# Last attention: moving the softmax divisors' reciprocals, their multiply from VectorE to GpSimd, and the first batch's output products by one group

## The chip, the cores and the metric

The kernel runs on one core of one Trainium2 chip. The time is the device time of one execution in microseconds (us); lower is better. Before the change three runs gave 2289.3, 2290.64 and 2291.68 us, median 2290.64.

## The reference

The program is a stack of four gated blocks, each a cross-attention and a feed-forward stage, on x of shape (2, 1024, 256). The change lies in the attention of the last block. There the roles are turned round: x, normalised, is the set of latents that asks, and the context (64 rows a batch) and x together are what is asked.

```
xn = layer_norm(x, ln_media_w, ln_media_b)      # the context, 2 x 64 x 256
zn = layer_norm(latents, ln_lat_w, ln_lat_b)    # x, 2 x 1024 x 256
q = (zn @ Wq).reshape(b, Nz, H, Dh)             # H = 8 heads, Dh = 64
kv_in = jnp.concatenate([xn, zn], axis=1)       # 1088 keys
k, v = kv_in @ Wk, kv_in @ Wv
sim = jnp.einsum('bhqd,bhfd->bhqf', q * scale, k)
alphas = jax.nn.softmax(sim, axis=-1)
out = jnp.einsum('bhqf,bhfd->bhqd', alphas, v)
return out.reshape(b, Nz, H * Dh) @ Wout
x = x + jnp.tanh(g_xattn[3]) * (that output)
```

## The kernel before, in words

The kernel has no scheduler: each engine has its own function, written in the order in which it runs, and semaphores tie them together. The last attention is `pe_xattn3` (TensorE), `act_xattn3` (ScalarE), `dve_xattn3` (VectorE) and `pool_xattn3` (GpSimd).

The work is cut into 16 groups G = 0 to 15. A group is one pair of heads p = G // 2 % 4 of one batch b = G // 8, for one half h = G % 2 of its 1024 queries (`block3`). A group has nine steps j = 0 to 8, one for each 128 keys (the last has 64). In a step:

- TensorE computes the scores of 128 keys by 512 queries for both heads (`pe_scores3`), a precise product in which the low parts of keys and queries take part, and the value product of the step two back (`pe_values3`), which gathers in bank 4. It also makes a rough product for the next group (`pe_rough3`), of which only the row maxima are used. The rough products of a group all use banks 5 and 6, so each waits until VectorE has reduced the one before (`s_ar`, line 2019).
- ScalarE takes the exponential (`act_weigh3`, line 2061), four buffers in turn.
- GpSimd adds the exponentials of the nine steps up (`pool_sum3`, lines 2089 and 2092): a step's sum starts when its exponential is there.
- VectorE reduces the rough product (`dve_rough3`, line 2019). At step 8 it makes the group's negated maxima out of them (`dve_maxima3`: line 2024, then two small multiplies at line 2026). TensorE turns those round (side work "m", "128x65" matmuls) before it can finish the next group's scores.

Beside this each step may carry one piece of side work, named by `side3(G, j)` and executed by all engines at that step: "s" at step 1 sums the exponentials of group G - 1 over the keys in bank 7, so that each query's divisor stands in every row, and ScalarE copies it to `x3_SM`; "q" at step 2 makes queries; "k" in even groups and "v" in odd ones at steps 3 to 5 make the next keys or values; "m" at step 8; "o" at steps 6 and 7 multiplies the finished outputs of a batch half by Wout, adds them to x and takes the statistics of the next layer norm. "q" and "k" bring VectorE two subtractions each, the low parts (line 1965); step 5 of an even group has short ones.

The divide is `dve_divide3`. `x3_RC` takes the reciprocals of group G - 1's divisors in four quarters of 128 columns, at steps 2 to 5 of group G (line 2074), and after the fourth one multiply of 128 x 512 elements scales the outputs in `x3_OE` in place (line 2080). Its semaphore `s_on` lets ScalarE write the next divisors and lets "o" start. "o" stands in groups 7, 8 and 15, each for the group before it, and after group 15 for group 15 itself.

VectorE's instructions at a step stand in this order: side work, rough reduce, reciprocal quarter, multiply. So what the multiply waits for, the next step's rough reduce waits for too, and behind it TensorE's next rough product.

Of the kernel before, what the change touches and what calls it, by code (L numbers as in the profile page):

```python
# [77 lines left out]
def build(nc, d, out):  # L78
    with ExitStack() as ctx:
# [647 lines left out]
        o = oR  # L727
# [1050 lines left out]
        def act_mid(e):  # L1778
            act_heads(e, 2)
            e.wait_ge(s_mk, 2)  # L1780
            for i in range(NT + 9):
# [32 lines left out]
                if 17 <= i < 23 and STAGES >= 7:  # L1814
# [14 lines left out]
        s_one = sem("ones_rows")  # L1829
        s_am, s_ar = sem("rough_scores"), sem("rough_maxima")  # L1830
        s_pa, s_oc = sem("keys_summed"), sem("values_kept")
        FIRST3 = [("k", 0, 0), ("k", 0, 1), ("q", 0, 0), ("v", 0, 0), ("v", 0, 1), ("q", 1, 0), ("k", 0, 2), ("v", 0, 2),
                  ("m", 0, 0)]
        FIRST_BANK3 = (0, 1, 2, 3, 0, 1, 7, 4, 7)

        def side3(G, j):

            n = G // 2
            if j == 1 and G:
                return ("s", G - 1, 0)  # L1840
            if j == 2 and G + 2 < 16:
                return ("q", G + 2, 0)
            if 3 <= j <= 5 and n + 1 < 8:
                return ("v" if G % 2 else "k", n + 1, j - 3)
            if 6 <= j <= 7 and G >= 7 and (G - 1) // 2 % 4 == 3:
                return ("o", G - 1, j - 6)
            if j == 8 and G + 1 < 16:
                return ("m", G + 1, 0)
            return None
# [70 lines left out]
        def act_side3(e, s):  # L1920
            kind, a, c = s
            if kind == "o":
                return
            bk = SIDE3_BANK[s]
            e.wait_ge(s_mi, SIDE3_AT[s] + 1)
            if kind == "k":
                for x in range(2):
                    e.activation(x3_K1[high3(x), a % 2, x, keys3(c)], psum[high3(x), bk, 0:512 if c < 2 else 64],
                                 ACT.Copy).then_inc(s_mo, 1)
                for x in range(2):  # L1930
                    e.wait_ge(s_mo, SIDE3_KEPT[s] - 3 + x)
                    e.activation(x3_K1[high3(1 - x), a % 2, x, keys3(c)], x3_K1[high3(x), a % 2, x, keys3(c)],
                                 ACT.Copy).then_inc(s_mo, 1)
            elif kind == "v":
                if c < 2:
                    m = e.activation(x3_VF[:, a % 2, 4 * c:4 * c + 4, :].rearrange("p x n -> p (x n)"), psum[:, bk, :],
                                     ACT.Copy)
                else:
                    m = e.activation(x3_VF[0:64, a % 2, 8, :], psum[0:64, bk, 0:128], ACT.Copy)
                m.then_inc(s_mo, 1)  # L1940
            elif kind == "q":
                for x in range(2):
                    e.activation(x3_Q1[high3(x), a % 3, x, :], psum[high3(x), bk, :], ACT.Copy).then_inc(s_mo, 1)  # L1943
                for x in range(2):
                    e.wait_ge(s_mo, SIDE3_KEPT[s] - 3 + x)
                    e.activation(x3_Q2[high3(x), a % 3, x, :], x3_Q1[high3(x), a % 3, x, :], ACT.Copy).then_inc(s_mo, 1)
            elif kind == "m":
                e.activation(x3_Q2[0:64, a % 3, 1, :], psum[0:64, bk, :], ACT.Copy).then_inc(s_mo, 1)
            else:
                if a:  # L1950
                    e.wait_ge(s_on, 40 + a)
                e.activation(x3_SM, psum[:, bk, :], ACT.Copy).then_inc(s_mo, 1)

        def dve_side3(e, s):
# [111 lines left out]
            e.wait_ge(s_pv, 40 + 9 * G + 9)  # L2066
            e.activation(x3_OE[:, p, 512 * h:512 * h + 512], psum[:, 4, :], ACT.Copy).then_inc(s_oc, 1)

        def dve_divide3(e, G, i):

            b, p, h = block3(G)
            if i == 0:
                e.wait_ge(s_mo, SIDE3_KEPT["s", G, 0])
            m = e.reciprocal(x3_RC[:, 128 * i:128 * i + 128], x3_SM[:, 128 * i:128 * i + 128])
            if i == 3 or (G, i) == (15, 1):
                c = slice(0, 512) if G < 15 else slice(128 * i - 128, 128 * i + 128)
                settle(e, dve, m)
                e.wait_ge(s_oc, G + 1)
                ov = x3_OE[:, p, 512 * h + c.start:512 * h + c.stop]
                e.tensor_tensor(ov, ov, x3_RC[:, c], ALU.mult).then_inc(s_on, 1)  # L2080

        def pool_sum3(e, G, j):
            g, rows = 9 * G + j, 128 if j < 8 else 64
# [69 lines left out]
        def dve_xattn3(e):  # L2153
# [8 lines left out]
            for G in range(16):  # L2162
                for j in range(9):
                    if j == 0 and G + 1 < 16:
                        dve_rough3(e, G + 1, 0)
                    if j == 8 and G + 1 < 16:
                        dve_maxima3(e, G + 1)
                    if side3(G, j):
                        dve_side3(e, side3(G, j))
                    if j < 8 and G + 1 < 16:  # L2170
                        dve_rough3(e, G + 1, j + 1)
                    if 2 <= j <= 5 and G:
                        dve_divide3(e, G - 1, j - 2)
            for i in range(4):
                dve_divide3(e, 15, i)
            for s in SIDE3[-2:]:
                dve_side3(e, s)

        def pool_xattn3(e):
# [7 lines left out]
            for G in range(16):  # L2187
                for j in range(1, 9):
                    pool_sum3(e, G, j)
                if G in (7, 8, 15):  # L2190
                    for i in range(2):
                        for t in tiles3(G - 1, i):
                            pool_rstd(e, 113 + t + 1, t)
            for i in range(2):
                for t in tiles3(15, i):
# [448 lines left out]
```

## Time and profile before

| | |
|---|---|
| median of three runs | 2290.64 us |
| the profiled execution's own time | 2299.54 us |
| its span, first to last instruction | 2297.6 us |
| TensorE matmul / weight load busy | 1812.1 us (79%) / 1123.4 us (49%) |
| VectorE busy | 1199.5 us (52%) |
| ScalarE busy | 879.3 us (38%) |
| GpSimd busy | 836.2 us (36%) |
| mean granted TensorE clock | 0.876 |
| the 16 groups of the last attention | from 1468.6 to some 2038 us |

The span is what the timeline is laid out on; the execution's own time is 1.9 us longer. It lies 0.4% over the median of the timed runs. A timeline row gives the start of an instruction (or of a merged run of like ones), how long it took, the engine, the line, what it writes and reads with shapes, how many were merged, and in square brackets how long its engine had been idle and whose end released it. fp32 matmuls appear as two instructions each. TensorE's ends are modelled; the distance from start to start is the reliable figure.

### The profile page before, as it was taken

The page shows a single profiled execution, that of the slowest core. Times are in us where ns is not written, and L with a number is a line of the kernel's source. Part 1 is how long each engine was busy: PE and PEld are TensorE (multiplying, and loading weights), DVE is VectorE, ACT ScalarE, POOL GpSimd, SP SyncE. Part 2 cuts the span into 40 slices and gives each one's busy share as a digit, 9 for nine tenths or more (in the row PEclk, how much of TensorE's full clock was granted, in tenths as well). Part 3 has the DMA queues.
Part 4 walks back from the last instruction along what each step waited for, and adds up shares of the span by engine and source line. Part 5 has one row for each costly group of instructions (what it writes and reads, how often), then busy time and mean ns, then how long its engine had stood idle before and what let it go on. Part 6 is the DMA issues. An engine that isn't in the chain of part 4 may idle for free.

```text
span 2297.6 us, 25602 instructions
## 1 busy us (share of the span) xinstructions
PE 1812.1 (79%) x9072; PEld 1123.4 (49%) x9072; DVE 1199.5 (52%) x2089; ACT 879.3 (38%) x1365; POOL 836.2 (36%) x805
## 2 busy tenths in 40 slices
PE   6744999818875788883997787899998999976895
PEld 3334889705653322262554355444454544463553
DVE  5932554354768467741113688555655565542334
ACT  3112443203236777720121455454553345410440
POOL 2133000062457444432001454555554555625014
PEclk9756999959977799985999888899998999977997
DMA  9112332120000000051112000000000000012343
GB/s 368 48 67 72 115 107 81 47 65 1 1 18 1 1 1 1 1 220 47 37 37 86 24 1 1 28 1 1 1 1 0 1 1 1 0 74 82 93 133 92
DMA packets 60075, 112.22 MB, mean 49 GB/s; under 512 B 7829, under 2 KB 51288, under 8 KB 57520
## 3 DMA queue, kind: packets, MB, share of 16 engines
q1 hardware_dynamic: 52272, 90.02, 11.2%
q0 software_dynamic: 7680, 20.57, 2.8%
q8 instruction: 76, 1.25, 0.2%
q14 instruction: 47, 0.39, 0.1%
HBM read 71.12 MB, written 39.80 MB: 48 GB/s over the span
## 4 chain that ended last, share of the span: by engine, by line
PE 61%; DVE 17%; POOL 8%; issue 5%; ACT 5%; DMA 2%; another core or an unknown queue 1%; SPq 0%; POOLq 0%; DVEq 0%; ACTq 0%
PE psum L149 57%; POOL arena L1519 2%; ACT arena L1318 2%; POOL arena L723 2%; POOL xb L718 2%; DVE arena L2080 2%; DVE arena L2019 1%; DVE arena L154 1%; PE psum L183 1%; DVE arena L164 1%; DVE arena L460 1%; DMA arena<-xb 1%; DVE arena L1400 1%; POOL arena L620 1%
## 5 line engine op out<-in xcount | busy, mean ns | idle before, releaser
L149 PE MATMUL psum<-arena 128*128 128x512 f32 (+20 forms) x5127 | 1230.0, 469 | 193.5 <-DVE arena L1434 30.6
L149 PEld LDWEIGHTS psum<-arena 128*128 128x128 f32 (+6 forms) x5127 | 603.7, 172 | 710.3 <-issue 471.2
L149 PE MATMUL psum<-rounded 128*128 128x270 f32 (+6 forms) x2688 | 486.8, 335 | 50.9 <-DVE arena L2019 24.4
L149 PEld LDWEIGHTS psum<-rounded 128*128 128x128 f32 (+3 forms) x2688 | 380.1, 188 | 162.1 <-DVE arena L2019 55.8
L2092 POOL TENSOR_TENSOR arena<-arena 128x1024 f32<-128x1024 f32 (+1 forms) x112 | 267.7, 2390 | 172.4 <-ACT arena L2061 170.7
L723 POOL DMA_INDIRECT arena<-yb,arena x80 | 78.3, 979 | 410.4 <-DMA yb<-arena 364.6
L2061 ACT ACTIVATE arena<-psum 128x1024 f32<-128x1024 f32 x144 | 147.2, 1022 | 208.4 <-PE psum L149 207.7
L2019 DVE TENSOR_REDUCE arena<-psum 128x1 f32<-128x1024 f32 x128 | 156.2, 1222 | 98.1 <-PE psum L149 96.9
L1318 ACT ACTIVATE arena<-psum,arena 128x1024 f32<-128x1024 f32 (+1 forms) x192 | 156.3, 909 | 46.4 <-PE psum L149 46.3
L1535 POOL TENSOR_TENSOR arena<-arena 128x256 f32<-128x256 f32 x128 | 94.1, 758 | 129.8 <-ACT arena L1318 129.0
L718 POOL DMA_INDIRECT xb<-arena x80 | 80.3, 1004 | 115.2 <-DVEq L2385 38.1
L191 ACT ACTIVATE arena<-psum 128x512 f32<-128x512 f32 x56 | 31.7, 596 | 215.2 <-PE psum L183 215.2
L183 PE MATMUL psum<-arena 128*128 128x128 f32 x224 | 42.7, 339 | 82.3 <-DVE arena L964 53.7
L759 DVE SCALAR_TENSOR_TENSOR rounded<-arena,rounded 128x540 fp32r<-128x540 f32 (+1 forms) x96 | 82.0, 886 | 33.6 <-ACT rounded L889 32.2
L883 ACT ACTIVATE arena<-psum,arena 128x540 f32<-128x540 f32 x64 | 45.4, 710 | 129.7 <-PE psum L149 126.9
L159 POOL TENSOR_SCALAR arena<-arena 128x1 f32<-128x1 f32 x113 | 24.4, 216 | 172.2 <-DVE arena L155 166.5
L183 PEld LDWEIGHTS psum<-arena 128*128 128x128 f32 x224 | 34.8, 187 | 91.1 <-DVE arena L964 54.2
L1965 DVE SCALAR_TENSOR_TENSOR rounded<-psum,rounded 64x512 fp32r<-64x512 f32 (+1 forms) x80 | 47.2, 590 | 60.5 <-ACT rounded L1943 47.4
L164 DVE TENSOR_SCALAR arena<-arena 128x256 f32<-128x256 f32 x128 | 61.3, 495 | 24.5 <-POOL arena L160 23.5
L2089 POOL TENSOR_TENSOR arena<-arena 128x1024 f32<-128x1024 f32 x16 | 38.0, 2377 | 84.3 <-ACT arena L2061 84.3
L160 POOL TENSOR_TENSOR arena<-arena 128x1 f32<-128x1 f32 x113 | 63.0, 557 | 9.4
L957 DVE TENSOR_TENSOR arena<-psum,arena 128x256 f32<-128x256 f32 (+1 forms) x40 | 16.9, 422 | 94.8 <-PE psum L149 94.8
(245 smaller groups left out, 1869.1 us busy)
## 6 DMA issues: line engine op xcount, KB each, us to landing
arena<-in_w SPq DMA_DIRECT2D x8, 2048.0 KB, 8.1
yb<-arena SPq DMA_DIRECT2D x102, 128.0 KB
xb<-arena SPq DMA_DIRECT2D x5, 2048.0 KB, 17.4
arena<-xb SPq DMA_DIRECT2D x70, 128.0 KB, 2.2
arena<-in_w1u SPq DMA_DIRECT2D x4, 2048.0 KB, 14.8
arena<-xb SPq DMA_DIRECT2D x8, 512.0 KB
arena<-in_w1d SPq DMA_DIRECT2D x1, 4096.0 KB, 13.8
arena<-in_w3b SPq DMA_DIRECT2D x1, 4096.0 KB, 12.4
```

The source lines that it names most:

```text
L149: return e.matmul(o, l, r, start=start, stop=stop, skip_group_check=True)
L160: e.tensor_tensor(RS[:, t:t + 1], VE[:, t:t + 1], cst("nhalf")[:, 0:1], ALU.pow).then_inc(s_rs, 1)
L164: e.tensor_scalar(xn(t), src(t), MV[:, t, 0:1], RS[:, t:t + 1], ALU.subtract, ALU.mult).then_inc(s_xn, 1)
L183: m = e.transpose(pt[:, t, k, :], src(2 * i + t)[:, 128 * k:128 * k + 128], ident)
L718: e.indirect_dma_start(buf, bass.IndirectOffsetOnAxis(idx[:, c:c + 1], 0), src(c % NT), None, bounds_check=bound, oob_is_err=False).then_i ...
L723: e.indirect_dma_start(dst, None, buf, bass.IndirectOffsetOnAxis(idx[:, col:col + 1], 0)).then_inc(s_gth[s], 16)
L759: e.scalar_tensor_tensor(out=dst, in0=src, scalar=1.0, in1=hi, op0=ALU.mult, op1=ALU.subtract).then_inc(sig, 1)
L1318: e.activation(PT[:, u % 3, 2 * h:2 * h + 2, 0:n], psum[:, bk:bk + 2, 0:n], ACT.Exp, bias=NBD[:, 0:1]).then_inc(s_ae, 1)
L1535: e.tensor_tensor(PT[:, u % 3, 2 * h:2 * h + 2, 0:128], PT[:, u % 3, 2 * h:2 * h + 2, 0:128], bc(cst("caus"), 1, 2), ALU.mult).then_inc(s_ ...
L2019: m = e.tensor_reduce(x3_MX[:, t, a, 0:1], psum[:, bk:bk + 2, :].rearrange("p c n -> p (c n)"), AX.X, ALU.max)
L2061: e.activation(x3_P[0:rows, g % 4].rearrange("p a n -> p (a n)"), psum[0:rows, bk:bk + 2, :].rearrange("p a n -> p (a n)"), ACT.Exp, scale ...
L2092: m = e.tensor_tensor(ac, ac, x3_P[0:rows, g % 4], ALU.add)
```

## The change

Three things are done. First, the quarters of the reciprocals are placed by a small table, `quarters3`: in odd groups at steps 3, 4, 5 and 6, in even groups one at step 5, two at step 6, one at step 7, in group 15 at steps 2 to 5. They are issued after the step's rough reduce as before, and each raises a new semaphore `s_rc3`. Second, the 128 x 512 multiply of groups 0 to 14 is done by GpSimd, after its sum of step 7 (in group 15 after that of step 5), when all four quarters and the values are there; GpSimd's sum of step 8 stands behind it. ScalarE may write the next divisors as soon as the quarters are made. The last group's divide stays on VectorE in two halves. Third, "o" for groups 6 and 7 stands in groups 8 and 9 and no longer in 7 and 8; that for group 14 stays in group 15.

```
-            if 6 <= j <= 7 and G >= 7 and (G - 1) // 2 % 4 == 3:
-                return ("o", G - 1, j - 6)
+            if 6 <= j <= 7 and G in (8, 9, 15):
+                return ("o", G - 1 if G == 15 else G - 2, j - 6)
...
-                    e.wait_ge(s_on, 40 + a)
+                    e.wait_ge(s_rc3, 4 * a)
...
+        def quarters3(G, j):
+
+            if G == 15:
+                return [j - 2] if 2 <= j <= 5 else []
+            if G % 2:
+                return [j - 3] if 3 <= j <= 6 else []
+            return [0] if j == 5 else [1, 2] if j == 6 else [3] if j == 7 else []
+
+        def dve_divisors3(e, G, i):
+
             if i == 0:
                 e.wait_ge(s_mo, SIDE3_KEPT["s", G, 0])
+                if G:
+                    e.wait_ge(s_on, 40 + G)
+            e.reciprocal(x3_RC[:, 128 * i:128 * i + 128], x3_SM[:, 128 * i:128 * i + 128]).then_inc(s_rc3, 1)
+
+        def pool_divide3(e, G):
+
+            b, p, h = block3(G)
+            e.wait_ge(s_rc3, 4 * G + 4)
+            e.wait_ge(s_oc, G + 1)
+            ov = x3_OE[:, p, 512 * h:512 * h + 512]
+            e.tensor_tensor(ov, ov, x3_RC, ALU.mult).then_inc(s_on, 1)
...
-                    if 2 <= j <= 5 and G:
-                        dve_divide3(e, G - 1, j - 2)
-            for i in range(4):
-                dve_divide3(e, 15, i)
+                    if G:
+                        for i in quarters3(G, j):
+                            dve_divisors3(e, G - 1, i)
+            for i in range(2):
+                dve_divisors3(e, 15, 2 * i)
+                dve_divisors3(e, 15, 2 * i + 1)
+                dve_divide3(e, i)
...
                 for j in range(1, 9):
                     pool_sum3(e, G, j)
-                if G in (7, 8, 15):
+                    if G and j == (5 if G == 15 else 7):
+                        pool_divide3(e, G - 1)
+                if G in (8, 9, 15):
```

VectorE's order in an even group (group 4), from the low parts of step 3 to the maxima, before:

```order
L1965 SCALAR_TENSOR_TENSOR rounded<-psum,rounded 64x512 x2
L2019 TENSOR_REDUCE arena<-psum 128x1
L2074 RECIPROCAL arena<-arena 128x128
L1965 SCALAR_TENSOR_TENSOR rounded<-psum,rounded 64x64 x2
L2019 TENSOR_REDUCE arena<-psum 128x1
L2074 RECIPROCAL arena<-arena 128x128
L2080 TENSOR_TENSOR arena<-arena 128x512
L2019 TENSOR_REDUCE arena<-psum 128x1 x2
L2024 TENSOR_REDUCE arena<-arena 128x8
L2026 TENSOR_SCALAR arena<-arena 128x4 x2
```

and after the change (here L1966 is the low parts, L2020 the rough reduce, L2084 a quarter of the reciprocals, L2025 and L2027 the maxima):

```order
L1966 SCALAR_TENSOR_TENSOR rounded<-psum,rounded 64x512 x2
L2020 TENSOR_REDUCE arena<-psum 128x1
L1966 SCALAR_TENSOR_TENSOR rounded<-psum,rounded 64x64 x2
L2020 TENSOR_REDUCE arena<-psum 128x1
L2084 RECIPROCAL arena<-arena 128x128
L2020 TENSOR_REDUCE arena<-psum 128x1
L2084 RECIPROCAL arena<-arena 128x128 x2
L2020 TENSOR_REDUCE arena<-psum 128x1
L2084 RECIPROCAL arena<-arena 128x128
L2025 TENSOR_REDUCE arena<-arena 128x8
L2027 TENSOR_SCALAR arena<-arena 128x4 x2
```

The multiply is gone from between the rough reduces; three of the quarters now stand behind it, and one between the last rough reduce and the maxima.

GpSimd's order in groups 14 and 15 before:

```order
L2089 TENSOR_TENSOR arena<-arena 128x1024
L2092 TENSOR_TENSOR arena<-arena 128x1024 x6
L2092 TENSOR_TENSOR arena<-arena 64x1024
L2089 TENSOR_TENSOR arena<-arena 128x1024
L2092 TENSOR_TENSOR arena<-arena 128x1024 x6
L2092 TENSOR_TENSOR arena<-arena 64x1024
```

and after (L2109 and L2112 are the sums, L2092 the multiply):

```order
L2109 TENSOR_TENSOR arena<-arena 128x1024
L2112 TENSOR_TENSOR arena<-arena 128x1024 x6
L2092 TENSOR_TENSOR arena<-arena 128x512
L2112 TENSOR_TENSOR arena<-arena 64x1024
L2109 TENSOR_TENSOR arena<-arena 128x1024
L2112 TENSOR_TENSOR arena<-arena 128x1024 x4
L2092 TENSOR_TENSOR arena<-arena 128x512
L2112 TENSOR_TENSOR arena<-arena 128x1024 x2
L2112 TENSOR_TENSOR arena<-arena 64x1024
```

The multiply stands before the last sum of a group, in group 15 before the last three.

## Rows read from the trace of the kernel before

**Rows 1.** Waits from 1465 to 2035 us: total us, times, longest.

```profile
PE psum L149 <- DVE arena L2019: 23.0, 20, 1.7
```

**Rows 2.** Busy by stretch, between two groups' first sums: length, engines, PEclk, DMA.

```profile
1602.75:1636.95 34.20, 31.75 (x126) 15.44 (x124) 21.96 (x26) 19.14 (x29) 19.16 (x8) 1.00 0.00 0
1636.95:1670.58 33.63, 31.58 (x150) 17.45 (x148) 19.24 (x20) 14.88 (x20) 19.13 (x8) 1.00 0.00 0
...
1704.78:1752.53 47.75, 41.49 (x182) 25.65 (x180) 24.20 (x32) 14.89 (x20) 21.83 (x16) 0.93 0.00 1
1752.53:1800.57 48.04, 41.35 (x158) 23.42 (x156) 26.92 (x38) 19.13 (x29) 21.84 (x16) 0.93 0.00 1
...
1834.19:1869.94 35.75, 33.27 (x126) 16.01 (x124) 21.96 (x26) 19.13 (x29) 19.16 (x8) 0.95 0.00 0
1869.94:1905.10 35.16, 33.10 (x150) 17.90 (x148) 19.24 (x20) 14.89 (x20) 19.12 (x8) 0.95 0.00 1
```

**Rows 3.** Timeline of group 5 (odd), steps 6 to 8.

```profile
1656.44 1.65 PE L149 MATMUL psum<-rounded 128*128 128x512 f32 x6
1656.63 2.38 POOL L2092 TENSOR_TENSOR arena<-arena 128x1024 f32<-128x1024 f32 x1 [0.65 <-ACT arena L2061]
1656.73 2.83 DVE L2080 TENSOR_TENSOR arena<-arena 128x512 f32<-128x512 f32 x1
...
1659.23 2.55 POOL L2092 TENSOR_TENSOR arena<-arena 128x1024 f32<-128x1024 f32 x1 [0.22 <-ACT arena L2061]
...
1660.75 1.67 PE L149 MATMUL psum<-rounded 128*128 128x512 f32 x6 [1.65 <-DVE arena L2019]
1661.52 1.23 DVE L2019 TENSOR_REDUCE arena<-psum 128x1 f32<-128x1024 f32 x1 [0.83 <-PE psum L149]
...
1662.98 0.24 DVE L2026 TENSOR_SCALAR arena<-arena 128x4 f32<-128x4 f32 x2
```

**Rows 4.** Timeline of group 4 (even), steps 6 to 8.

```profile
1622.71 0.95 DVE L2074 RECIPROCAL arena<-arena 128x128 f32<-128x128 f32 x1
...
1622.77 1.67 PE L149 MATMUL psum<-rounded 128*128 128x512 f32 x6
...
1625.58 2.56 POOL L2092 TENSOR_TENSOR arena<-arena 128x1024 f32<-128x1024 f32 x1 [0.21 <-ACT arena L2061]
...
1627.11 1.67 PE L149 MATMUL psum<-rounded 128*128 128x512 f32 x6 [1.66 <-DVE arena L2019]
...
1629.34 0.24 DVE L2026 TENSOR_SCALAR arena<-arena 128x4 f32<-128x4 f32 x2
```

**Rows 5.** Timeline of group 7, whose steps 6 and 7 carry "o".

```profile
1727.50 6.69 PE L149 MATMUL psum<-arena 128*128 128x256 f32 x16 [3.16 <-DVE arena L2080]
1733.84 1.74 PE L149 MATMUL psum<-rounded 128*128 128x512 f32 x6
...
1739.89 1.75 PE L149 MATMUL psum<-rounded 128*128 128x512 f32 x6
...
1742.76 2.33 POOL L2092 TENSOR_TENSOR arena<-arena 64x1024 f32<-64x1024 f32 x1 [3.70 <-ACT arena L2061]
...
1743.58 1.61 DVE L2026 TENSOR_SCALAR arena<-arena 128x4 f32<-128x4 f32 x2
...
1745.34 1.06 PE L149 MATMUL psum<-arena 128*65 128x128 f32 x8 [2.70 <-DVE arena L2026]
```

**Rows 6.** GpSimd's groups by shape: count, busy us, mean ns, idle before.

```profile
L2092 POOL TENSOR_TENSOR arena<-arena 128x1024 f32<-128x1024 f32 x96 | 230.1, 2397 | 139.0 <-ACT arena L2061 137.3
L1535 POOL TENSOR_TENSOR arena<-arena 128x256 f32<-128x256 f32 x128 | 94.1, 758 | 129.8 <-ACT arena L1318 129.0
```

**Rows 7.** Timeline of group 15 and of the last "o".

```profile
2002.71 12.68 POOL L2092 TENSOR_TENSOR arena<-arena 128x1024 f32<-128x1024 f32 x5 [0.78 <-ACT arena L2061]
...
2004.54 1.11 DVE L2080 TENSOR_TENSOR arena<-arena 128x512 f32<-128x512 f32 x1
...
2010.07 4.73 PE L149 MATMUL psum<-arena 128*64 128x512 f32 x20
...
2014.44 1.28 PE L149 MATMUL psum<-rounded 128*128 128x512 f32 x4
...
2029.05 9.56 PE L149 MATMUL psum<-arena 128*128 128x256 f32 x32 [3.04 <-DVE arena L2080]
```

More of the change, by code:

```diff
@@ L1831, in build @@
         s_pa, s_oc = sem("keys_summed"), sem("values_kept")
+        s_rc3 = sem("divisors_made")
         FIRST3 = [("k", 0, 0), ("k", 0, 1), ("q", 0, 0), ("v", 0, 0), ("v", 0, 1), ("q", 1, 0), ("k", 0, 2), ("v", 0, 2),
@@ L2067, in act_values3, with dve_divide3 @@
             e.activation(x3_OE[:, p, 512 * h:512 * h + 512], psum[:, 4, :], ACT.Copy).then_inc(s_oc, 1)
-        def dve_divide3(e, G, i):
-            b, p, h = block3(G)
+        def quarters3(G, j):
[5 more added lines that the diff above has]
+        def dve_divisors3(e, G, i):
             if i == 0:
                 e.wait_ge(s_mo, SIDE3_KEPT["s", G, 0])
[L2074 to L2080, printed above, removed]
+                if G:
[7 more added lines that the diff above has]
+            e.tensor_tensor(ov, ov, x3_RC, ALU.mult).then_inc(s_on, 1)
+        def dve_divide3(e, i):
+            b, p, h = block3(15)
+            e.wait_ge(s_rc3, 4 * 15 + 2 * i + 2)
+            e.wait_ge(s_oc, 16)
+            ov = x3_OE[:, p, 512 * h + 256 * i:512 * h + 256 * i + 256]
+            e.tensor_tensor(ov, ov, x3_RC[:, 256 * i:256 * i + 256], ALU.mult).then_inc(s_on, 1)
         def pool_sum3(e, G, j):
@@ L2189, in pool_xattn3 @@
                     pool_sum3(e, G, j)
-                if G in (7, 8, 15):
+                    if G and j == (5 if G == 15 else 7):
+                        pool_divide3(e, G - 1)
+                if G in (8, 9, 15):
                     for i in range(2):
-                        for t in tiles3(G - 1, i):
+                        for t in tiles3(G - 1 if G == 15 else G - 2, i):
                             pool_rstd(e, 113 + t + 1, t)
```

## The prediction

> **What bounds the kernel now.** I read the page first, then the busy times by stretch, the waits, and the timeline of a few groups.
>
> In the last attention TensorE is the bound: in a group of 33.6 to 34.2 us it is busy 31.6 to 31.8, VectorE 19 to 22, GpSimd 19 [rows 2]. What it loses, it loses to VectorE: 23.0 us in 20 waits behind the rough reduce [rows 1]. The timeline shows why. In group 5 TensorE starts the seventh rough product at 1656.44; I call this moment R7. The multiply starts at 1656.73 and takes 2.83 us, because GpSimd began a sum at 1656.63, 0.10 us earlier, and ended it at 1659.01. The reduce behind it is late, and the eighth rough product (R8) starts at 1660.75 after 1.65 us of idleness [rows 3]. Group 4 has the same, R7 at 1622.77, R8 at 1627.11 after 1.66 us [rows 4]. So a group loses about 1.7 us there.
>
> What TensorE does after R8: the maxima (line 2026) end at 1662.98 + 0.24 = 1663.22, and in group 7 the "m" matmul follows 0.15 us behind them (1743.58 + 1.61 = 1745.19, then 1745.34) [rows 3, 5]. So "m" starts at 1663.37, R8 + 2.62, and R7 + 6.93. In group 4 it is 1629.58 + 0.15 = 1629.73, R7 + 6.96. Without the stall R8 would come at R7 + 2.6 (my estimate: 4.31 and 4.34 from R7 to R8 less the idle 1.65 and 1.66, rounded to TensorE's own 2.6) and "m" at R7 + 5.2. That is the yardstick: 6.93 and 6.96 now, 5.2 at best.
>
> **Odd groups.** The multiply leaves VectorE; a quarter (0.95 us, as in [rows 4]) stands behind the seventh reduce, which starts 0.77 us after R7 and takes 1.23 [rows 3]: R7 + 2.95, before the eighth product at + 3.37 is ready for its reduce. That costs nothing. The maxima would start at R8 + 2.23 = R7 + 4.83. But GpSimd's sum of step 7 starts at R7 + 2.79 (1659.23) and, without the multiply of VectorE that stretched it to 2.55, takes 2.38, until R7 + 5.17 [rows 3]. The maxima's two multiplies can't run beside it: in group 7 they took 1.61 us in place of 0.24 and ended 0.10 after the GpSimd sum (1742.76 + 2.33 = 1745.09) [rows 5]. So they end at R7 + 5.27 and "m" starts at R7 + 5.42. Gain: 6.93 - 5.42 = 1.51 us. I assume here that VectorE gets in between two GpSimd instructions that stand back to back. The row that bears on it: the multiply at 2004.54 took 1.11 us and ended at 2005.65, while GpSimd ran five sums in 12.68 us without a pause; had it waited for a second sum it would have taken over 3 [rows 7].
>
> **Even groups.** The first quarter is at 1622.71 as now, until 1623.66; the seventh reduce then runs until 1624.90, two quarters until 1626.77, the eighth reduce (ready at R7 + 2.6 + 0.77 = 1626.14) until 1628.0, the fourth quarter until 1628.97, R7 + 6.20. Line 2026 would follow at + 0.24. But GpSimd has ended its sum of step 7 (1625.58 + 2.38 = 1627.96) and waits for just this quarter; it starts its multiply some 0.1 us after it, ahead of line 2026, and holds it off as the sum that began 0.10 us ahead held off the multiply in [rows 3]. The multiply's price on GpSimd is in no row. Bounds: 0.76 us (a quarter of the elements of the sum, line 1535) and 2.40 (the whole sum) [rows 6]; on the line between them 512 columns cost 1.3, which I take, since both rows are the same operation kind with two inputs. Then "m" starts at R7 + 6.20 + 0.1 + 1.3 + 0.25 = R7 + 7.85. Loss: 0.89 us against now (0.35 to 2.0 at the bounds). TensorE stands idle 2.6 us there.
>
> The Trainium skill ("SBUF — State Buffer", Who interferes with whom) says that VectorE and GpSimd share a port pair as an exclusive lock, that whoever issues first keeps it for the whole instruction, and that a reduce never contends. The trace agrees on both points: 2.83 us above, and reduces of 1.23 us beside a running sum. Were only the order of issue to change in even groups, VectorE first, the loss would go; this is the first rival below.
>
> **The "o" groups.** In groups 7 and 8 "o" waits for the multiply, 3.16 us idle in group 7 [rows 5], and then runs slowly: 16 matmuls from 1727.50 to R7 at 1733.84, 6.34 us, where the same 16 and four value matmuls took 4.37 in group 15 (2010.07 to 2014.44) [rows 7], that is 3.37 without the four (1.0, my estimate from TensorE's rate there). 2.97 us more: the row of that stretch shows a clock of 0.93 [rows 2], so part of it ran at 1.2 GHz in place of 2.4. After the change "o" reads outputs of two groups back: no wait, no slow stretch.
> The stretches now: 47.75 + 48.04 and a plain odd one, 33.63: 129.4 us [rows 2]. After: group 7 plain, 33.63 - 1.51 = 32.1. Group 8: 34.20 - 1.75 (R8 at its natural place) + 2 x 3.37 + the idleness at "m". There the fourth quarter stands between reduce and maxima: R8 + 3.46 + 0.95 = 4.41, GpSimd's multiply until 5.8, "m" at R8 + 6.05, idle 3.4: 42.6. It is as long as the waits behind which the clock fell in three of three cases (3.16, its twin in group 8, 3.04 in [rows 7]), so + 1.5. Group 9: 33.63 - 1.7 + 6.74 + 2.8 (as now at "m", where R8 1739.89 to 1745.34 is 5.45 less 2.62) = 41.5. Sum 117.7, gain 11.7.
>
> **Group 15.** Here GpSimd is the late one: five sums back to back, 12.68 us from 2002.71, the steps of TensorE shorter than a sum [rows 7]. The quarters are made early, but the multiply stands behind the sum of step 5: 2002.71 + 4 x 2.38 + 3 x 0.14 = 2012.65, + 0.14 + 1.3 = 2014.1. "o" is wanted at 2010.07 + 1.0 = 2011.1 and now starts at 2014.25: idle 3.15 us, and by the three cases the 16 matmuls run slowly, + 2.97. Loss 6.1. The last divide is as before.
>
> **The clock.** Three plain stretches are 1.5 to 1.6 us longer than their like, of which the last two are shown: 35.75 and 35.16 with a clock of 0.95 against 34.20 and 33.63 with 1.00 [rows 2]. They are groups whose 1.65 us wait at R8 ended in a short low clock. These waits go: - 4.7. The even groups get a wait of 2.6 us in their place; waits of 1.65 lowered the clock in 3 of 13 plain groups, those of 2.70 at "m" in none of 2. I take 2 of 6: + 3.1.
> By the Trainium skill ("TensorE: Matmul & The Clock Gate", HAM oscillation) only longer gaps of idleness matter; by that the + 3.1 would be nought and the sum 3 us lower. The trace disagrees in part, with its 0.95 behind gaps of 1.65.
>
> **The sum.** Odd groups 1, 3, 5, 11, 13: 5 x -1.51 = -7.6. Even 2, 4, 6, 10, 12, 14: 6 x 0.89 = +5.3. Groups 7 to 9: -11.7. Clock: -4.7 + 3.1. Group 15: +6.1. Together -9.5 us. The profiled execution took 2299.54 us (span 2297.6) and would take 2290.0; it lies 8.9 over the median of the timed runs, which have the same instructions and, I suppose, fewer low clocks. From the median: 2290.6 - 9.5 = 2281.
>
> **Rivals.**
> 1. VectorE's maxima come ahead of GpSimd's multiply, or this is near its lower bound, and few low clocks come: even groups 6.96 - 6.85 = -0.1 each (fourth quarter 6.20 + 0.24 + 0.24 + 0.15 = 6.83), 6 us better, group 8 too 2, no new low clocks -3, group 15 at full clock -3 at most: 2268 to 2274. For it: 0.1 us decides. Against: in [rows 3] 0.10 us was enough for GpSimd.
> 2. Every even group's 2.6 us wait lowers the clock: four more at 1.55, 6 us, and the multiply nearer 1.6 than 1.3 us, 2: 2288 to 2290, no change that can be told. For it: a wait of 1.65 can do it. Against: none of 2 at 2.70.
> 3. Slower: GpSimd's own next instruction takes the ports before VectorE's waiting one. Then the multiply, ready at once in odd groups, holds the maxima off too: "m" at R7 + 5.17 + 0.1 + 1.3 + 0.25 = 6.8, the gain of six odd groups 0.1 in place of 1.5, + 8; with a low clock behind each such wait of 1.6 (6 x 1.55) and rival 2's 6: 2281 + 23 = 2304, or without half of the low clocks 2296. It decides from the first odd group on. Against: the 1.11 us of [rows 7].
> 4. The change does not do what it says: GpSimd's multiply delays its own sums so that exponentials wait. Against: before a group's first sum GpSimd idles 3 to 5 us (19 busy of 34 [rows 2]), and four buffers lie between. It would give 2286 to 2290; I count it with rival 2.
>
> **Chances.** Forecast 0.50 (2275 to 2286), rival 1 0.20, rivals 2 and 4 0.20, rival 3 0.10. 0.2% (4.6 us) is about what a measurement of this kernel can tell from no change. Faster by more: forecast and rival 1, and a little of 2, less a little of the forecast: 0.72. Within: 0.20. Slower: 0.08. Range 2269 to 2289: rival 1's fast end and rival 3 are left out.
>
> **What would show it.** Right: in odd groups no TensorE idleness at R8, "m" 5.4 us after R7, line 2027 ending 0.1 behind a GpSimd sum; in even groups "m" 7.8 after R7, line 2027 stretched to some 1.3 us behind GpSimd's 128 x 512 multiply, and TensorE idle 2.6 before it; "o" without a wait in groups 8 and 9, with one of 3 us in group 15. Wrong: a line 2027 of 0.24 us in even groups (rival 1); PEclk of 0.95 in each even stretch (rival 2); line 2027 held in odd groups past the multiply (rival 3). A GpSimd multiply of 2 us would move the even groups to a loss of 1.6 each and take half of the gain.

## The result and the profile after

The changed kernel took 2274.91 us, median of four runs (2268.78 to 2277.72), against 2290.94 for the kernel before (four runs, 2289.30 to 2291.68): a ratio of 0.9927, 95% interval 0.9911 to 0.9943. Run again on another chip, the ratio was 0.9953 (0.9928 to 0.9978). It is faster, by less than 1%; the forecast was 2281, its range 2269 to 2289. One execution of a later run (all four edits together) took 3377 us against 2257.56 to 2267.23 in its five others; it is left out of that run's time and ratio.

The profiled execution took 2268.78 us (span 2266.6). The page's busy times, share of the span and instructions:

```profile
PE 1811.5 (80%) x9072; PEld 1125.2 (50%) x9072; DVE 1167.7 (52%) x2074; ACT 879.7 (39%) x1365; POOL 852.3 (38%) x820
```

15 multiplies left VectorE (2089 to 2074 instructions, 1199.5 to 1167.7 us) and came to GpSimd (805 to 820, 836.2 to 852.3 us). TensorE's work is the same.

Profile against profile, the span fell by 31.0 us, twice what the medians say. So I cut the spans in three: what stands ahead of the last attention (1468.58 us before, 1472.03 after), the last attention, from its first sum to the first matmul of the last turn, and what follows. First the kernel before, then a second profile of it, then after; columns as in [rows 2]:

```profile
1468.58:2041.30 572.72, 525.64 (x2197) 279.26 (x2195) 325.65 (x395) 257.49 (x350) 317.07 (x159) 0.97 0.02 8
2041.30:2297.60 256.30, 188.56 (x781) 124.21 (x781) 85.67 (x220) 62.25 (x167) 62.57 (x65) 0.83 0.29 90
```
```profile
2047.73:2282.80 235.07, 185.41 (x781) 123.81 (x781) 85.63 (x220) 62.46 (x167) 62.55 (x65) 0.86 0.32 98
```
```profile
1472.03:2030.90 558.87, 523.86 (x2197) 279.99 (x2195) 294.04 (x380) 257.46 (x350) 332.98 (x174) 0.98 0.02 8
2030.90:2266.60 235.70, 185.14 (x781) 123.84 (x781) 85.88 (x220) 62.58 (x167) 62.57 (x65) 0.86 0.32 98
```

The kernel before took 256.30 us for its last part in one execution and 235.07 in the other. Those 21 us are no effect of the change. The part ahead of the attention, which the change doesn't touch, wanders too: from 1468.6 to 1482.0 us over the twelve profiles of this document. The 31.0 us are 13.9 in the attention, 20.6 in the last part, less 3.5 ahead. The attention is the clean measure: 572.72 us before and 572.85 in its second profile; 558.87 after and 558.87 in its second. The change gave **13.9 us** there; 9.5 were forecast. The medians differ by 16.0; where the other 2 lie can't be told, as both outer parts wander by more.

Where they came from, by stretch (groups 3, 4, 8, 9, 12 and 14 of after; group 7 is as long as group 3, 32.09):

```profile
1569.51:1601.60 32.09, 31.53 (x150) 17.48 (x148) 16.71 (x19) 14.89 (x20) 20.16 (x10) 1.00 0.00 1
1601.60:1635.95 34.35, 31.70 (x126) 15.45 (x124) 20.43 (x25) 19.13 (x29) 20.23 (x9) 1.00 0.00 0
...
1734.48:1776.95 42.47, 38.59 (x158) 21.54 (x156) 24.12 (x37) 19.12 (x29) 23.11 (x17) 1.00 0.00 0
1776.95:1821.16 44.21, 41.49 (x182) 25.33 (x180) 21.40 (x31) 14.88 (x20) 23.07 (x17) 0.92 0.00 1
...
1887.58:1923.03 35.45, 33.18 (x126) 16.63 (x124) 20.43 (x25) 19.14 (x29) 20.22 (x10) 0.95 0.00 0
...
1955.11:1983.07 27.96, 26.09 (x100) 12.35 (x98) 13.84 (x15) 10.97 (x13) 20.22 (x9) 0.94 0.00 1
```

An odd group went from 33.63 us [rows 2] to 32.09, with TensorE idle for some 0.56 us of it in place of 2.05. An even one went from 34.20 to 34.35. The three stretches that held "o" and its neighbour summed to 129.4; they are 32.09 + 42.47 + 44.21 = 118.77.

**An odd group.** The timeline of group 3, steps 6 to 8, which answers to [rows 3]:

```profile
1589.00 1.65 PE L149 MATMUL psum<-rounded 128*128 128x512 f32 x6
...
1591.59 1.67 PE L149 MATMUL psum<-rounded 128*128 128x512 f32 x6
1591.79 2.38 POOL L2112 TENSOR_TENSOR arena<-arena 128x1024 f32<-128x1024 f32 x1 [0.22 <-ACT arena L2062]
...
1593.82 0.45 DVE L2027 TENSOR_SCALAR arena<-arena 128x4 f32<-128x4 f32 x2
1594.13 1.26 POOL L2092 TENSOR_TENSOR arena<-arena 128x512 f32<-128x512 f32 x1
1594.42 1.06 PE L149 MATMUL psum<-arena 128*65 128x128 f32 x8 [0.15 <-DVE arena L2027]
```

R8 comes at R7 + 2.59 with no idleness; "m" at R7 + 5.42. Line 2027, ready at 1593.82, ended at 1594.27, 0.10 behind the end of the sum (1591.79 + 2.38 = 1594.17), with GpSimd's multiply next in its queue. The first of its two instructions started at 1593.82, beside the sum, and took 0.38; the second took 0.16 and was not held by the multiply: VectorE got in between the two.

**An even group.** Group 2, which answers to [rows 4]:

```profile
1555.18 1.65 PE L149 MATMUL psum<-rounded 128*128 128x512 f32 x6
1555.95 1.23 DVE L2020 TENSOR_REDUCE arena<-psum 128x1 f32<-128x1024 f32 x1 [0.29 <-PE psum L149]
1557.10 1.75 DVE L2084 RECIPROCAL arena<-arena 128x128 f32<-128x128 f32 x2
1557.78 1.67 PE L149 MATMUL psum<-rounded 128*128 128x512 f32 x6
...
1558.77 1.16 DVE L2020 TENSOR_REDUCE arena<-psum 128x1 f32<-128x1024 f32 x1
1559.85 0.94 DVE L2084 RECIPROCAL arena<-arena 128x128 f32<-128x128 f32 x1
...
1560.84 1.32 DVE L2027 TENSOR_SCALAR arena<-arena 128x4 f32<-128x4 f32 x2
1560.86 1.27 POOL L2092 TENSOR_TENSOR arena<-arena 128x512 f32<-128x512 f32 x1 [0.50 <-DVE arena L2084]
1562.31 1.06 PE L149 MATMUL psum<-arena 128*65 128x128 f32 x8 [1.85 <-DVE arena L2027]
```

The multiply starts 0.07 us after the fourth quarter (1560.79) and two small instructions of 128 x 4 values take 1.32 us beside it: the first, which starts some 0.02 us ahead of the multiply, 0.17, the second 1.24. TensorE stands for 1.85 us.

**The "o" groups and group 15** of after:

```profile
1769.75 1.06 PE L149 MATMUL psum<-arena 128*65 128x128 f32 x8 [3.08 <-DVE arena L2027]
...
1809.54 1.60 DVE L2027 TENSOR_SCALAR arena<-arena 128x4 f32<-128x4 f32 x2
...
1811.29 1.06 PE L149 MATMUL psum<-arena 128*65 128x128 f32 x8 [2.70 <-DVE arena L2027]
...
1986.22 9.93 POOL L2112 TENSOR_TENSOR arena<-arena 128x1024 f32<-128x1024 f32 x4 [0.77 <-ACT arena L2062]
...
1996.10 1.26 POOL L2092 TENSOR_TENSOR arena<-arena 128x512 f32<-128x512 f32 x1
...
1997.51 6.59 PE L149 MATMUL psum<-arena 128*128 128x256 f32 x16 [2.86 <-POOL arena L2092]
2003.75 1.28 PE L149 MATMUL psum<-rounded 128*128 128x512 f32 x4
```

"o" no longer waits in groups 8 and 9; "m" does, 3.08 and 2.70 us. In group 15 "o" waits 2.86 us for the multiply behind four sums, and then runs slowly (6.24 us to the next row's start, against the 3.37 worked out from [rows 7]).

By wait, over the whole attention of after (total us, times, longest), against 23.0 us in 20 waits in [rows 1]:

```profile
PE psum L149 <- DVE arena L2027: 17.7, 13, 3.1
```

The waits behind the rough reduce are nearly gone (2.7 us in 7). 17.7 us of waits stand now in front of "m".

### The profile page after: what moved, and what is told of

Same layout as the page of the kernel before. It is cut to its first block, busy times and chain, and to the rows that moved or that the text cites. A ratio compares the mean times of both kernels' runs of the same rounds, so it can differ in the third digit from the quotient of the medians.

```text
span 2266.6 us, 25617 instructions
## 1 busy us (share of the span) xinstructions
PE 1811.5 (80%) x9072; PEld 1125.2 (50%) x9072; DVE 1167.7 (52%) x2074; ACT 879.7 (39%) x1365; POOL 852.3 (38%) x820
## 4 chain that ended last, share of the span: by engine, by line
PE 62%; DVE 16%; POOL 9%; issue 5%; ACT 5%; DMA 2%; SPq 0%; POOLq 0%; DVEq 0%; ACTq 0%
PE psum L149 58%; POOL xb L718 3%; POOL arena L1519 2%; POOL arena L723 2%; DVE arena L2020 2%; ACT arena L1318 2%; PE psum L183 1%; DVE arena L154 1%; DVE arena L164 1%; DVE arena L460 1%; DMA arena<-xb 1%; DVE arena L1400 1%; DVE arena L2084 1%; POOL arena L620 1%; DVE arena L2027 1%
## 5 line engine op out<-in xcount | busy, mean ns | idle before, releaser
L149 PE MATMUL psum<-arena 128*128 128x256 f32 (+19 forms) x5127 | 1228.1, 468 | 184.8 <-DVE arena L1434 31.1
L149 PEld LDWEIGHTS psum<-arena 128*128 128x128 f32 (+5 forms) x5127 | 603.0, 172 | 698.0 <-issue 460.1
L2112 POOL TENSOR_TENSOR arena<-arena 128x1024 f32<-128x1024 f32 (+1 forms) x112 | 265.5, 2370 | 137.5 <-ACT arena L2062 136.0
L2020 DVE TENSOR_REDUCE arena<-psum 128x1 f32<-128x1024 f32 x128 | 156.0, 1220 | 106.0 <-PE psum L149 104.9
L183 PE MATMUL psum<-arena 128*128 128x128 f32 x224 | 42.6, 339 | 82.4 <-DVE arena L964 53.9
L1966 DVE SCALAR_TENSOR_TENSOR rounded<-psum,rounded 64x512 fp32r<-64x512 f32 (+1 forms) x80 | 47.6, 595 | 74.8 <-ACT rounded L1944 47.4
L2109 POOL TENSOR_TENSOR arena<-arena 128x1024 f32<-128x1024 f32 x16 | 38.0, 2376 | 81.0 <-ACT arena L2062 81.0
## 6 DMA issues: line engine op xcount, KB each, us to landing
xb<-arena SPq DMA_DIRECT2D x5, 2048.0 KB, 17.7
arena<-in_w1d SPq DMA_DIRECT2D x1, 4096.0 KB, 13.7
```

What stands on the lines that cost most here:

```text
L149: return e.matmul(o, l, r, start=start, stop=stop, skip_group_check=True)
L183: m = e.transpose(pt[:, t, k, :], src(2 * i + t)[:, 128 * k:128 * k + 128], ident)
L2020: m = e.tensor_reduce(x3_MX[:, t, a, 0:1], psum[:, bk:bk + 2, :].rearrange("p c n -> p (c n)"), AX.X, ALU.max)
L2112: m = e.tensor_tensor(ac, ac, x3_P[0:rows, g % 4], ALU.add)
```

## The experiments

The change has three parts: the outputs a group later, the multiply on GpSimd, and new places of the quarters. The attention's length is given for each beside the ratio, since it doesn't contain the wandering parts ahead of it and behind it. Each attention length is that of one profiled execution.

**The outputs alone** (the kernel before, "o" moved; multiply and quarters stay on VectorE as they were).

```
-            if 6 <= j <= 7 and G >= 7 and (G - 1) // 2 % 4 == 3:
-                return ("o", G - 1, j - 6)
+            if 6 <= j <= 7 and G in (8, 9, 15):
+                return ("o", G - 1 if G == 15 else G - 2, j - 6)
```

> Before, with the first batch's output products in groups 8 and 9 instead of 7 and 8 and nothing else. Theory: two waits of 3.2 us and two slow stretches of 3.0 us go (12.3), and group 7 gets the plain stall of 1.7: 10.6 us less than before, 2280. VectorE's multiply is hidden in groups 8 and 9 behind the output products. Rival (the gain is the multiply's new engine): within 3 us of before.

Measured: 2276.27 us, ratio 0.9929 (0.9903 to 0.9954), attention 558.76 us, 14.0 less than before. That is 3.4 us more than expected, and 3.1 of it are low clocks that this run lacks in groups 2 and 11 (34.21 and 33.64 us against 35.81 and 35.16). Group 2 stands ahead of anything that the edit changes, and in the second profile of the kernel before it has no low clock either: which groups have one can differ from execution to execution (last section). Plain groups keep 33.63 and 34.21 us and their stall:

```profile
PE psum L149 <- DVE arena L2019: 22.8, 19, 1.7
```

Groups 7 to 9 take 33.63 + 43.01 + 41.54 = 118.2 us. VectorE's slow multiply lies beside the 20 matmuls that hold "o" there and costs nothing:

```profile
1767.43 4.73 PE L149 MATMUL psum<-arena 128*64 128x512 f32 x20
...
1769.38 2.19 DVE L2080 TENSOR_TENSOR arena<-arena 128x512 f32<-128x512 f32 x1
```

So this part alone is worth as much as the whole change, give or take the few us of low clocks. The other two together must come to about nought.

**The multiply on GpSimd, with the quarters left early** (the changed kernel, one quarter at each of steps 2 to 5 in every group).

```
 def quarters3(G, j):
-    if G == 15:
-        return [j - 2] if 2 <= j <= 5 else []
-    if G % 2:
-        return [j - 3] if 3 <= j <= 6 else []
-    return [0] if j == 5 else [1, 2] if j == 6 else [3] if j == 7 else []
+    return [j - 2] if 2 <= j <= 5 else []
```

> After, with the quarters of the reciprocals at steps 2 to 5 in every group, as before the change. Theory (the even groups lose at the maxima because the last quarter releases GpSimd's multiply just when the maxima want the ports): in even groups the maxima wait only for the end of the sum of step 7 and 'm' comes 5.4 us after R7 in place of 7.13, 1.7 us in six groups and 0.4 in group 8, some 10.5 us less than after: 2264. Rival (quarters belong where no low parts are): TensorE waits at steps 3 to 5 of even groups for the low parts, 0.5 to 1 us a step: 2280 or more.

Measured: 2257.14 us, ratio 0.9854 (0.9830 to 0.9877), attention 542.13 us: 16.6 less than with the outputs alone, 16.7 less than the whole change, where 10.5 were expected. Its group 2:

```profile
1563.70 1.68 PE L149 MATMUL psum<-rounded 128*128 128x512 f32 x6
...
1566.51 2.39 POOL L2108 TENSOR_TENSOR arena<-arena 128x1024 f32<-128x1024 f32 x1 [0.21 <-ACT arena L2062]
...
1568.55 0.45 DVE L2027 TENSOR_SCALAR arena<-arena 128x4 f32<-128x4 f32 x2
1568.86 1.27 POOL L2088 TENSOR_TENSOR arena<-arena 128x512 f32<-128x512 f32 x1
1569.15 1.06 PE L149 MATMUL psum<-arena 128*65 128x128 f32 x8 [0.17 <-DVE arena L2027]
```

Now an even group reads as an odd one: the multiply is ready before the sum of step 7 ends, line 2027 gets in ahead of it, and "m" comes at R7 + 5.45. An even group takes 32.65 us (after: 34.34), an odd one 32.1 as in the changed kernel, and no plain group shows a low clock any more. So in these profiles the multiply's move gives 16.6 us, and the quarters' new places take 16.7 back. The 6.2 beyond the expected lie where the clock differs: 4.9 in groups 9, 12 and 14, whose low clocks are gone, and 2.4 in group 15, whose quarters stand in the same places in both kernels and whose clock is 0.92 here and 0.85 in the changed kernel; less 1.15 in group 8 (clock 0.96, 0.75 longer where 0.4 less was expected). In odd groups the places change nothing; in even ones they put the multiply's start beside line 2027.

**The quarters' places alone** (the outputs moved and the new places, but the multiply on VectorE, directly behind the fourth quarter).

```
+def quarters3(G, j):        # the table of the changed kernel
-                    if 2 <= j <= 5 and G:
-                        dve_divide3(e, G - 1, j - 2)
+                    if G:
+                        for i in quarters3(G, j):
+                            dve_divide3(e, G - 1, i)
```

> The kernel with only the output products moved, plus the new places of the quarters; the multiply stays on VectorE, behind the fourth quarter. Theory: the fourth quarter in even groups ends 5.6 us after R7, the sum of step 8 begins at 5.4 and holds the multiply off until 7.75, 'm' at 8.9 in place of 6.96; in odd groups the multiply meets the sum of step 7 and ends at 5.7, 'm' at 7.45 in place of 6.93: some 15 us over the run with the output products moved alone, 2291. Rival (a step without low parts is the better place by itself): 2277 or less.

Measured: 2328.31 us, ratio 1.0074 (1.0045 to 1.0103), attention 589.96 us: 31.2 more than with the outputs alone, where 15 were forecast. Its group 4:

```profile
1641.46 1.68 PE L149 MATMUL psum<-rounded 128*128 128x512 f32 x6
...
1647.11 2.65 DVE L2088 TENSOR_TENSOR arena<-arena 128x512 f32<-128x512 f32 x1
...
1650.25 1.89 PE L149 MATMUL psum<-arena 128*65 128x128 f32 x8 [3.51 <-DVE arena L2026]
```

"m" stands at R7 + 8.79, close to the 8.9 expected. Two things were missed. One is the clock: behind waits of 3.5 us the matmuls of "m" take 1.89 us in place of 1.06, and the attention's mean clock is 0.96 against 0.99 with the outputs alone; all six plain even groups and three of the six odd ones have a low clock. The other is in the odd groups: "m" comes at R7 + 8.16, not 7.45, since line 2026 meets the sum of step 8 and is held until that ends. Group 5:

```profile
1683.49 2.52 POOL L2100 TENSOR_TENSOR arena<-arena 64x1024 f32<-64x1024 f32 x1 [0.22 <-ACT arena L2061]
...
1685.19 0.92 DVE L2026 TENSOR_SCALAR arena<-arena 128x4 f32<-128x4 f32 x2
```

So the new places cost whichever engine multiplies, and far more if it is VectorE.

**The last multiply early** (the changed kernel, in group 15 the multiply in front of the sum of step 3 in place of step 5).

```
-if G and j == (5 if G == 15 else 7):
+if G and j == (3 if G == 15 else 7):
```

> After, with GpSimd's multiply in group 15 behind the sum of step 3 in place of step 5. Theory: the wait of 2.86 us before the output product of group 14 and the slow 16 matmuls behind it (6.2 in place of 3.4 us) both go: 5.7 us less than after, 2269. Rival (the slow stretch has another cause): only 2.9 us less.

Measured: 2269.84 us, ratio 0.9906 (0.9881 to 0.9930), attention 552.04 us, 6.8 less than after. In group 15:

```profile
2001.01 1.30 POOL L2092 TENSOR_TENSOR arena<-arena 128x512 f32<-128x512 f32 x1
...
2003.50 4.73 PE L149 MATMUL psum<-arena 128*64 128x512 f32 x20
```

"o" neither waits nor runs slowly (20 matmuls in 4.73 us, as in [rows 7]); the stretch from group 15's first sum to the last turn is 40.99 us in place of 47.8. That confirms the cause of the largest single loss of the change.

**The maxima without multiplies** (the changed kernel; the same numbers from two reduces that negate, each of one half, written where the multiplies wrote).

```
-            settle(e, dve, e.tensor_reduce(x3_M1, x3_MX, AX.X, ALU.max))
             for a in range(2):
-                m = e.tensor_scalar(x3_NM[:, :, 64 * (1 - a)], x3_M1[:, :, a], -1.0, None, ALU.mult)
+                m = e.tensor_reduce(x3_NM[:, :, 64 * (1 - a)], x3_MX[:, :, a, :], AX.X, ALU.max, negate=True)
```

> After, with the negated maxima made by two reduces straight into their place, instead of one reduce and two small multiplies behind it. Theory (the two small multiplies are held off by whatever GpSimd runs, and a reduce is not): in even groups 'm' comes 6.05 us after R7 in place of 7.13, in odd groups 5.2 in place of 5.4, in groups 8 and 9 1.1 and 1.5 us earlier; 10 us less than after, the attention 549 us long in place of 558.9. Rival (what holds 'm' is the reciprocal in front, or TensorE's own queue): within 2 us of after.

Measured: 2277.52 us against 2309.80 for the kernel before on that chip, ratio 0.9862 (0.9836 to 0.9888), attention 541.88 us: 17.0 less than after, 10 expected. Its group 6:

```profile
1690.44 1.67 PE L149 MATMUL psum<-rounded 128*128 128x512 f32 x6
...
1695.97 0.17 DVE L2026 TENSOR_REDUCE arena<-arena 128x4 f32<-128x8 f32 x2
1696.13 1.27 POOL L2091 TENSOR_TENSOR arena<-arena 128x512 f32<-128x512 f32 x1 [0.49 <-DVE arena L2083]
1696.28 1.06 PE L149 MATMUL psum<-arena 128*65 128x128 f32 x8 [0.56 <-DVE arena L2026]
```

Both maxima take 0.17 us and are done by the time GpSimd's multiply starts, since they have one instruction fewer ahead of them; so an even group doesn't show whether a reduce would be held off. "m" stands at R7 + 5.84 in place of 7.13. Group 9 shows it, where a sum is running:

```profile
1808.29 2.35 POOL L2111 TENSOR_TENSOR arena<-arena 64x1024 f32<-64x1024 f32 x1 [2.44 <-ACT arena L2061]
1808.91 0.23 DVE L2026 TENSOR_REDUCE arena<-arena 128x4 f32<-128x8 f32 x2
...
1809.29 1.06 PE L149 MATMUL psum<-arena 128*65 128x128 f32 x8 [1.12 <-DVE arena L2026]
```

The two multiplies took 1.60 us in that place. Even groups take 33.04 us, odd ones 31.89, group 8 41.17, group 9 39.95. Six even groups at 1.30, six odd ones at 0.2, group 8 at 1.30, group 9 at 4.26 (its low clock gone) and the low clocks of groups 12 and 14, 2.3, make 16.9 us. So nearly all of it hung on a few multiplies of 128 x 4 values that GpSimd held off; the instruction that fell away is the smaller part.

**Short sums on GpSimd** (the kernel before; the first sum of each group is an addition of a constant to one tile, the others read 64 of 1024 columns, so the divisors leave most keys out).

```
-m = e.tensor_tensor(ac, x3_P[:, (g - 1) % 4], x3_P[:, g % 4], ALU.add)
+m = e.tensor_scalar(ac, x3_P[:, g % 4], 1.0, None, ALU.add)
...
-m = e.tensor_tensor(ac, ac, x3_P[0:rows, g % 4], ALU.add)
+m = e.tensor_tensor(ac[:, :, 0:32], ac[:, :, 0:32], x3_P[0:rows, g % 4, :, 0:32], ALU.add)
```

> Before, with GpSimd's sums over 64 columns in place of 1024 (the first of each group adds 1 to the exponentials instead), so the divisors leave out most keys. Theory (VectorE's multiply is long only because a GpSimd sum holds the ports): the 128x512 multiply takes 0.69 us in place of 2.2 to 2.8, the stall at R8 goes in odd groups (33.62 us to 31.9) and shrinks to 0.3 in even ones (34.20 to 32.75), 'o' waits 1.1 us in place of 3.2 and its slow stretch goes: attention 536 us, time 2254. Rival (two tiles read and one written in place make it long): multiply over 2 us still, time within 5 us of before.

Measured: 2264.43 us, ratio 0.9816 (0.9780 to 0.9853), attention 532.76 us, 536 expected. VectorE's multiply by line (shortest, median and longest in ns), and its place in group 5:

```profile
L2080 DVE TENSOR_TENSOR arena<-arena x17: 424/693/775, 1522.6 to 1996.5; 128x512 f32<-128x512 f32 x15, 128x256 f32<-128x256 f32 x2
```
```profile
1651.61 0.32 POOL L2092 TENSOR_TENSOR arena<-arena 128x64 f32<-128x64 f32 x1 [2.70 <-ACT arena L2061]
1651.70 0.78 DVE L2080 TENSOR_TENSOR arena<-arena 128x512 f32<-128x512 f32 x1
```

The same multiply in the same place takes 0.78 us where [rows 3] show 2.83, and the stall at R8 is gone. Nothing was moved. So the 1.7 us of a plain group were contention with the sums, not the multiply's own work.

**All four together** (outputs, multiply on GpSimd, early quarters, the last multiply at step 3, the maxima by reduces), run on two chips.

> After, with quarters at steps 2 to 5 everywhere, the multiply of group 15 behind the sum of step 3, and the maxima by two reduces. Theory: the attention of the run with early quarters (542.1 us) less 4.4 us in group 15, less 0.2 us in each of twelve groups, less 1.5 us in groups 8 and 9: 532 us, time 2247. Rival (the gains overlap): 2252 or more.

> The kernel with all four edits once more, beside after on one chip. Theory: attention 532 us, 27 less than after; ratio to before 0.981, to after 0.988. Rival (its gain depends on the chip): ratio to before 0.986 or more.

Measured: 2264.85 us (median of five) against 2309.80, ratio 0.9804 (0.9775 to 0.9833); and 2241.09 against 2288.37, ratio 0.9803 (0.9779 to 0.9827). The attention takes 531.68 and 531.75 us; 532 was forecast. This version beats both kernels: 41 us less in the attention than before, 27 less than after.

**The kernels unchanged, again.**

> The kernel before, unchanged, for a second profile. Theory: the first 2030 us are as in the first profile (last attention 560.5 us from its first sum to the last output product), and the last feed-forward stage, 268.5 us in the first profile of before against 248.3 in that of after, varies from execution to execution by some 10 us for reasons outside the change: here 255 to 262 us, span near 2289. Rival: the change itself shortens the feed-forward stage (its first part meets another phase of the weight transfer): then before shows 266 us or more again.

> After, unchanged, on another occasion. Theory: the attention is again 559 us long within 3 (which groups fall into a low clock may change), plain odd groups 32.1 and even ones 34.3 us, group 15 47.8, and the time 0.993 of before. Rival (the first profile of after was a lucky one): attention 564 us or more.

Measured: 2284.59 us in one execution, attention 572.85; and 2276.19 (2275.09 to 2276.83), attention 558.87. The attention's length repeats to 0.13 us or better. The last part's doesn't: of twelve profiles it took 233 to 237 us in seven and 252 to 256 in five: the four profiles from the chip on which the kernel before took 2309.80, and the first profile of the kernel before.

## Why the prediction was right, and where it was off

The prediction named what bounds a group before and after, and the wait that would replace the old one; these held. Its sum was 4.4 us short in the attention.

- **Odd groups**, -1.51 us each forecast. 33.62 to 32.11 us, "m" at R7 + 5.42: exact, -7.6 in five groups.
- **GpSimd's multiply**, taken at 1.3 us between bounds of 0.76 and 2.40. It took 1.262 to 1.277 in 15 cases. The line between two sizes of the same operation was enough.
- **Even groups**, +0.89 us each forecast: this is the mis-sized term. They went from 34.20 to 34.34, so +0.8 us in place of +5.3. The mechanism was as told: multiply directly behind the fourth quarter, line 2027 held (1.32 us; first instruction let in, second held), TensorE idle before "m" (1.85 us; 2.6 forecast). What I had too late was the fourth quarter's end: it lies at R7 + 5.61, not 6.20. Only 0.13 of these 0.59 us come from the start: I let the first quarter stand where its [rows 4] twin stood, at R7 - 0.06; with the quarters out of steps 2 to 4 it stands at R7 - 0.47, and the seventh reduce starts at R7 + 0.77, not 0.90. The other 0.46 come from adding up VectorE's instructions by their durations. Back to back each starts some 0.1 us before the one ahead ends, so two quarters, a reduce and a quarter took 3.61 us from the seventh reduce's end (1557.18) to 1560.79, not 4.07. From there to "m" it was 1.52 us in place of 1.65: the multiply followed in 0.07, took 1.27, and what stands behind it 0.18. That line 2027 is held at all, and that the reduces of the experiment are not, is as the Trainium skill has it ("SBUF — State Buffer", Who interferes with whom: the first to issue keeps the ports, a reduce never contends); the traces agree: the multiply that started behind GpSimd's took 1.24 us, and beside a sum two reduces took 0.23 us where two multiplies took 1.60.
- **Groups 7 to 9**, -11.7 forecast, -10.6 measured. Group 8 took 42.47 us (42.6), but without the low clock that I added apart; group 9 44.21 (41.5), with a low clock (0.92) behind its wait of 2.70 us.
- **The clock**, -4.7 + 3.1 forecast. The three slow plain stretches went; groups 12 and 14 got new ones (clock 0.95 and 0.94, +1.1 and +1.2): -4.7 + 2.3. That waits of 2.70 leave the clock alone, "none of 2", fell with group 9. The "3 of 13" that waits of 1.65 us lowered are 3 of 12: group 0 has no such wait. By the Trainium skill ("TensorE: Matmul & The Clock Gate", HAM oscillation), which lets only longer gaps of idleness count, the 2.3 would have been nought; the rows of 0.95 and 0.94, in groups whose wait before "m" was 1.85 us, disagree.
- **Group 15**, +6.1 forecast: 41.74 to 47.82, +6.08. The run with the multiply at step 3 gave 6.8 back.
- **Sum**: -7.6 + 0.8 - 10.6 - 4.7 + 2.3 + 6.1 = -13.7, against 13.9 measured in the attention; 9.5 were forecast. The even groups account for 4.5 of the difference, the clock for 0.8, and groups 7 to 9 take 1.1 back.
- **From the median**, not from the profiled execution: that choice held. The execution was 8.9 us over the median, and its last part was 21 us over that of the next one; from it the forecast would have been 2290. The reason given, fewer low clocks, is not the one: the attention took 572.72 and 572.85 us in the two profiles, and the difference lies outside it.
- **What was luck**: the 2274.91 lies 6 us under the forecast, 4.4 by the attention and the rest by the outer parts. These wander by 13 and 23 us from profile to profile, more than the 12 us from the forecast to the fast end of the range, and the working has no term for that.

Rival 1 would give line 2027 0.24 us in even groups: its number for the time came near, its mechanism did not. Rival 2, a low clock in every even stretch, had two of six. Rival 3, VectorE passed over between two instructions of GpSimd, is excluded by each odd group (line 2027 done 0.10 us behind the sum). Rival 4: no wait for exponentials came up among TensorE's.

By parts: outputs -14.0, multiply on GpSimd -16.6, the quarters' places +16.7 (even groups 6 x 1.69 = 10.1, group 15 2.4, groups 9, 12 and 14 with their low clocks 2.7, 1.1 and 1.15, less 0.75 in group 8). Each is a difference of two profiles in which other groups may have a low clock, worth some 1.5 us a group. The prediction never priced the last two apart; that they nearly cancel, it did not know.

## What to carry to other kernels

Where VectorE and GpSimd both work on SBUF beside a busy TensorE, look at which of VectorE's instructions stand in front of what TensorE waits for, and keep them from starting beside a long GpSimd one: move the long one, make it ready before the sum ahead of it ends, or put the small one as a reduce, or let it come first. Try each part of such a change alone; here one part took back what another gave. And when instructions are taken out of early steps, work out anew where the later ones start, rather than keep the times of the trace of before; and add up instructions that stand back to back by their distances from start to start, not by their durations.

## What the runs showed of the hardware that I had not expected

- Size does not protect. Two VectorE multiplies of 128 x 4 values took 0.24 us alone, 1.32 beside GpSimd's 128 x 512 multiply and 1.60 beside a sum. As two reduces they took 0.23 us beside a sum, and the attention gained 17.0 us by that one edit.
- A waiting VectorE instruction gets in at the release. With GpSimd's instructions back to back, line 2027 was over 0.10 us behind the end of GpSimd's sum in each of the six odd groups, and GpSimd's multiply behind that sum was hardly delayed: it ended 1.22 us after the sum's end (1594.13 + 1.26 against 1594.17). In even groups the first multiply of line 2027 starts at nearly the same moment as GpSimd's (1560.84 and 1560.86) and isn't held, while the second, issued 0.07 us behind GpSimd's, takes 1.24 us.
- A low clock comes behind waits of quite different length, and not always. In the same attention a wait of 3.08 us brought none, one of 2.70 a row of 0.92; before, waits of 1.65 us lowered it in three of the 12 plain groups that have one. In part it is chance: the second profile of the kernel before has it in group 9 (35.85 us) and not in group 2 (34.19), the first the other way round (33.62 and 35.81), and its groups 7 and 8 take 46.41 and 48.94 us in place of 47.75 and 48.04. The sums still agree to 0.13 us, and the two profiles of the changed kernel have it in the same groups. What decides it stays open.
- The last part of the kernel has two lengths, 20 us apart, with a clock of 0.83 to 0.85 in the long one and 0.86 to 0.87 in the short one and VectorE's work the same (85.67 and 85.63 us in the two profiles of before). It goes neither with the change nor wholly with the chip. The cause stays open; it is why the comparison was made on the attention. The part ahead of the attention wanders by up to 13 us (1468.6 to 1482.0), also without a known cause.
